# First layer of a two-layer transformer kernel: the gates' arithmetic moved ahead of the first projections, the query blocks ahead of the gate blocks, both running sums together, and the wait for a trip through DRAM left to one queue

## The reference

```
h  = layernorm(x) * (1 + ca) + sa
q, k, v, gate = h @ Wq.T, h @ Wk.T, h @ Wv.T, h @ Wg.T     # 32 query heads, 8 key heads, D = 128; rope on q and k
dt = softplus(h @ Win.T + dt_bias);  g = -dt * exp(A_log_bias)
G  = cumsum(g) inside chunks of 128 tokens
y_intra = (q k^T * causal * exp(G_i - G_j)) (v dt)
state   = state * exp(G_last) + (k exp(G_last - G))^T (v dt)
y_inter = (q exp(G)) state_before
y = rmsnorm(y_intra + y_inter) * gnorm_w * silu(gate);  out = y @ Wo.T
```

## Time and profile before

| What | us |
|---|---|
| median of 3 runs | 1562.36 |
| the three runs | 1556.58, 1562.36, 1563.45 |
| the profiled execution | 1558.13 |
| its span | 1556.3 |

### The profile page before, as it was taken

One profiled execution on the slowest core, in us unless ns is written; L12 is line 12 of the kernel. 1 busy time (PEld: TensorE's weight loads), 2 busy tenths in 40 slices (PEclk: granted clock), 3 DMA queues, 4 the chain that ended last, 5 costly groups with the idle time before them and its releaser, 6 DMA issues. The chain is left out here.

```text
span 1556.3 us, 18582 instructions
## 1 busy us (share of the span) xinstructions
PE 1270.4 (82%) x6079; PEld 896.2 (58%) x6079; DVE 997.4 (64%) x1723; ACT 630.2 (40%) x1177; POOL 736.0 (47%) x742
## 2 busy tenths in 40 slices
PE   4869999999999999999999999776989999951000
PEld 2647767767776777777777777565853334330000
DVE  6635565655655566556656565676578888437888
ACT  2333433433333433433433433245327767734223
POOL 0255755656655756756756756656200012041007
PEclk9989999999999999999999999989868989965555
DMA  4212122122113121121121121120654310000001
GB/s 155 70 49 62 41 76 68 55 69 81 55 55 94 43 69 51 59 68 48 61 69 52 57 68 43 46 95 1 129 109 70 58 38 2 2 1 0 0 0 54
DMA packets 70552, 86.47 MB, mean 56 GB/s; under 512 B 6853, under 2 KB 40805, under 8 KB 69882
## 3 DMA queue, kind: packets, MB, share of 16 engines
q1 hardware_dynamic: 68586, 82.57, 19.6%
q10 hardware_dynamic: 1872, 2.72, 0.5%
HBM read 77.49 MB, written 7.51 MB: 55 GB/s over the span
## 5 line engine op out<-in xcount | busy, mean ns | idle before, releaser
L1657 POOL TENSOR_TENSOR sw<-sw,sinT 128x512 f32<-128x512 f32 x80 | 103.0, 1287 | 153.4 <-ACT sw L1390 153.4
L1190 DVE TENSOR_REDUCE nm<-banks 128x2 f32<-128x1024 f32 x128 | 152.1, 1219 | 33.4 <-PE banks L747 32.8
L1439 ACT ACTIVATE yTh<-yF 128x512 fp32r<-128x512 f32 x64 | 40.4, 631 | 319.2 <-DVE yF L1042 319.2
L1669 POOL TENSOR_TENSOR dec<-gb,gcol 128x512 f32<-128x512 f32 x64 | 70.8, 1107 | 206.7 <-DVE Sd L1008 197.5
L1545 ACT ACTIVATE Pb<-banks 128x512 f32<-128x512 f32 x256 | 135.0, 602 | 52.7 <-PE banks L768 52.2
L545 PE MATMUL banks<-hTh,wgh 128*128 128x512 f32 x256 | 122.5, 479 | 0.0
L980 DVE SCALAR_TENSOR_TENSOR gs<-tg,banks 128x512 f32<-128x512 f32 x64 | 44.0, 687 | 120.8 <-ACT tg L1397 120.8
L597 PE MATMUL banks<-st,qt 128*128 128x128 f32 x384 | 82.4, 299 | 37.1 <-DVE Sd L1008 21.1
L545 PE MATMUL banks<-hTh,wqh 128*128 128x512 f32 x256 | 108.0, 422 | 0.0
L625 PE MATMUL banks<-woh,yTh 128*128 128x512 f32 x256 | 105.0, 410 | 3.5 <-DVE yTl L1045 3.5
L545 PE MATMUL banks<-hTh,wql 128*128 128x512 f32 x256 | 101.7, 397 | 0.0
(11 more groups left out here) (307 smaller groups left out, 3410.4 us busy)
## 6 DMA issues: line engine op xcount, KB each, us to landing
gb<-g_scr SPq DMA_DIRECT2D x64, 256.0 KB, 3.5
raw<-in_wmod SPq DMA_DIRECT2D x40, 256.0 KB, 2.7
raw<-in_wo SPq DMA_DIRECT2D x32, 256.0 KB, 2.9
raw<-in_wq SPq DMA_DIRECT2D x31, 256.0 KB, 2.7
raw<-in_wg SPq DMA_DIRECT2D x31, 256.0 KB, 2.7
qsT<-q_scr SPq DMA_DIRECT2D x24, 256.0 KB, 6.7
q_scr<-hl SPq DMA_DIRECT2D x32, 128.0 KB, 4.3
mt<-mods_scr SPq DMA_DIRECT2D x12, 256.0 KB, 4.9
```

Source lines behind the costliest of these rows:

```text
L1190: ve.tensor_reduce(nm[:, b, i, p:32:16], pairs[z_][:, :].rearrange("p (g t) -> p g t", g=2), AX.X, ALU.max, negate=True).then_inc(*v_nm.up ...
L1657: po.tensor_tensor(s_[:, :], s_[:, :], sinT[:, :], ALU.mult).then_inc(*g_rope.up("sin", kind, t, n))
L1669: po.tensor_tensor(dec[:, :, :], gb[s % 2][:, :, :], bc(gcol[:, t % 2, heads(t), n], 2, 128), ALU.subtract).then_inc(*g_dec.up("sub", s))
```

## The change

The gates are called before the first projections rather than two steps behind one another, so they stand earlier in each queue, above all in DVE's. The query blocks of group 0 come ahead of its gate blocks; gate blocks 2 and 3 go into slot 0. Both running sums are made in one step, with the second in bank 4. The barrier `loop_start` goes on all five engines (DVE's stands for them in the diff): SP waits for the DRAM writes ahead of `load_gb(0)` and `load_gb(4)`, and POOL waits for `gcol`, `dtc` and `cxd` where it reads them. Two instructions add the bias in place of eight. Slot 0 is written out by itself, and the four splits of the output weights go into it. The list of `group_order(0)` follows the new order.

```
     def group_order(g):
         if g == 0:
-            return [("k", 0), ("q", 0), ("v", 0), ("g", 0), ("q", 1), ("g", 1), ("q", 2), ("g", 2), ("q", 3), ("g", 3),
+            return [("k", 0), ("q", 0), ("v", 0), ("q", 1), ("q", 2), ("q", 3), ("g", 0), ("g", 1), ("g", 2), ("g", 3),
+    gbank = (5, 4)
...
-                for i in range(NT):
-                    v = ve.tensor_tensor(z[:, i // 4, :, i % 4], banks[5][:, i * 32:(i + 1) * 32], dtb[:, :], ALU.add)
+                for b in range(2):
+                    v = ve.tensor_tensor(z[:, b, :, :].rearrange("p h n -> p n h"), banks[5][:, b * 128:(b + 1) * 128].rearrange("p (n h) -> p n h", n=4),
+                                         bc(dtb[:, :], 1, 4), ALU.add)
...
-        def loop_start(self):
-            ve = self.e
-            ve.wait_ge(*v_dt("cxd"))
-            ve.wait_ge(*d_gs[0](0))
-            ve.wait_ge(*d_gs[1](0))
...
         def prep(self, s):
             po.wait_ge(*d_gb[s % 2](s))
+            if s == 0:
+                po.wait_ge(*v_dt("gcol", 1))
...
         def load_gb(self, s):
             sp, t, n = self.e, s // 4, s % 4
+            if s in (0, 4):
+                sp.wait_ge(*d_gs[t](0))
...
     def first_pieces(E):
+        E.gate(0), E.gate(1)
+        E.piece("k", 0, 0)
+        E.gate(2)
+        E.split()
+        E.gate(3), E.gate(4)
+        E.piece("q", 0, 0)
+        E.gate(5)
+        E.split()
+        E.piece("v", 0, 0)
+        E.turn_k(0)
+        E.gate(6), E.gate(7)
+        E.piece("q", 0, 1)
+        E.turn_v(0)
+        E.prep2(0, ("xc",))
+        E.split()
+        E.piece("q", 0, 2)
+        E.gsum()
+        E.split()
+        E.piece("q", 0, 3)
+        E.gcols()
+        E.load_gb(0), E.load_gb(1)
+        E.split()
+        E.prep(0)
+        E.piece("g", 0, 0)
+        E.state_cols()
+        E.prep_exp(0)
+        E.prep2(0, ("xd",))
+        E.split()
+        E.piece("g", 0, 1)
+
+    def first_slot(E):
+        E.scores(0)
+        E.prep(1)
+        E.piece("g", 0, 2)
+        E.outputs(0)
+        E.norm_a(0)
+        E.prep_exp(1)
+        E.norm_pow(0)
+        E.piece("g", 0, 3)
+        E.split(), E.split()
+        E.piece("q", 1, 0)
+        E.state(0)
+        E.load_gb(2)
+        E.norm_b(0)
+        E.piece("g", 1, 0)
+        E.split(), E.split()
+        E.piece("k", 1, 0)
+        E.prep2(1)
```

More of the change, by code:

```diff
@@ L511, in z_turn, with gsum, gcols @@
             mm.then_inc(*p_head.up("zT"))
[L513 to L522, removed]
-            pe = self.e
+        def gsum(self):
+            pe = self.e
+            for b in range(2):
+                pe.wait_ge(*v_dt("g", b))
+                pe.transpose(banks[gbank[b]][:, 0:128], zz[:, b, :, :].rearrange("p h n -> p (h n)"), ident).then_inc(*p_head.up("gT", b))
+        def gcols(self):
+            pe = self.e
+            for b in range(2):
+                pe.wait_ge(*v_dt("gsum", b))
+                pe.transpose(banks[gbank[b]][:, 128:256], gT[b][:, :], ident).then_inc(*p_head.up("gcol", b))
             for b in range(2):
@@ L925, in gate @@
                                             op0=ALU.mult, op1=ALU.mult).then_inc(*v_dt.up("g", b))
[L926 to L944, removed]
@@ L946, in gtot, with gsum @@
-        def gtot(self, part):
-            ve = self.e
[L948 to L956, removed]
-            ve = self.e
-            ve.wait_ge(*v_dt("cxd"))
-            ve.wait_ge(*d_gs[0](0))
-            ve.wait_ge(*d_gs[1](0))
+        def gsum(self):
+            ve = self.e
+            for b in range(2):
+                iv = gT[b][:, :].rearrange("p (a c) -> p a c", c=16)
+                ve.wait_ge(*p_head("gT", b))
+                ve.tensor_copy(gin[b][:, :], banks[gbank[b]][:, 0:128]).then_inc(*v_dt.up("gin", b))
+                ve.wait_ge(*v_dt("gin", b))
+                ve.tensor_tensor_scan(gT[b][:, :], rst[:, :], gin[b][:, :], 0.0, ALU.mult, ALU.add).then_inc(*v_dt.up("scan", b))
+                ve.wait_ge(*v_dt("scan", b))
+                ve.tensor_copy(gtot[b][:, 0:8], iv[:, :, 15]).then_inc(*v_dt.up("ends", b))
+                ve.wait_ge(*v_dt("ends", b))
+                ve.tensor_tensor_scan(gtot[b][:, 8:16], rst[:, 1:9], gtot[b][:, 0:8], 0.0, ALU.mult, ALU.add).then_inc(*v_dt.up("upto", b))
+                ve.wait_ge(*v_dt("upto", b))
+                ve.tensor_tensor(iv[:, 1:8, :], iv[:, 1:8, :], bc(gtot[b][:, 8:15], 2, 16), ALU.add).then_inc(*v_dt.up("gsum", b))
@@ new lines, in gcols, with state_cols @@
+        def gcols(self):
+            ve = self.e
+            for b in range(2):
+                ve.wait_ge(*p_head("gcol", b))
+                ve.tensor_copy(gcol[:, b, :, :].rearrange("p h n -> p (h n)"), banks[gbank[b]][:, 128:256]).then_inc(*v_dt.up("gcol", b))
+            ve.wait_ge(*p_head("gtot"))
+            ve.wait_ge(*v_dt("gcol", 1))
+            ve.tensor_tensor(bhn(ww), banks[7][:, 0:256], bhn(gcol), ALU.subtract).then_inc(*v_dt.up("tot"))
+        def state_cols(self):
+            ve = self.e
+            ve.wait_ge(*a_head("tot"))
+            ve.tensor_tensor(bhn(cxd), bhn(ww), bhn(dtc), ALU.mult).then_inc(*v_dt.up("cxd"))
@@ L1853, in send_tile, with gsum @@
             sp.dma_start(raw[k % NRAW][:, :], weight_src(k)).then_inc(*d_raw[k % NRAW].up(k))
-        def gsum(self, b):
+        def gsum(self):
             sp = self.e
[L1857 to L1864, removed]
+            for b in range(2):
+                sp.wait_ge(*v_dt("gsum", b))
+                sp.dma_start(d_g[b], gT[b][:, :]).then_inc(*d_gs[b].up(0))
         def load_gb(self, s):
             sp, t, n = self.e, s // 4, s % 4
+            if s in (0, 4):
+                sp.wait_ge(*d_gs[t](0))
             if s >= 2:
@@ L2348, in layer0_head @@
         E.z_turn()
-        ahead = stream(E, first_pieces)
-        for part in range(8):
-            E.gate(part)
-            if part < 7:
-                ahead.step(), ahead.step()
-        for b in range(2):
-            E.gsum(b)
-            ahead.step(), ahead.step()
-        E.gtot(0)
-        ahead.step(), ahead.step()
-        E.gtot(1)
-        ahead.rest()
-        E.loop_start()
-    def layer0_loop(E):
-        E.load_gb(0), E.load_gb(1)
-        E.prep(0), E.prep_exp(0), E.prep2(0)
-        for _ in range(4):
-            E.split()
-        for s in range(NSLOT - 4):
+    def layer0_loop(E):
+        first_pieces(E)
+        first_slot(E)
+        for s in range(1, NSLOT - 4):
             t, n = s // 4, s % 4
```

52 lines of the change are left out of this document (14 added, 38 removed).

## The result

| | before | changed |
|---|---|---|
| median us (runs) | 1561.83 (4) | 1540.65 (4) |
| lowest, highest | 1556.58, 1563.45 | 1534.91, 1543.67 |
| profiled execution, its span | 1558.13, 1556.3 | 1540.01, 1538.2 |

The ratio is 0.9866, interval 0.9828 to 0.9903: 21 us less, and between 15 and 27. The forecast was 10.3 us less, 1552, range 1545 to 1560.

What follows compares the result with a forecast made beforehand. PE was taken as the bound, busy 82% of the span, with waits and half-speed clock in the head. Removed 20.2, put back 9.7, rounding 0.2: gain 10.3 us, 1562.4 to 1552; range 1545 to 1560, likeliest 1548 to 1556.

Steps and rivals of the forecast that it cites:

- DVE up to the key: Before the key's cos product: reciprocal and one multiplication move into DVE's 2.06 us idle gap; cost nothing.
- From the key to g and the sums: DVE's gate chain in the head, held up by POOL: g at 60.2, first sum at 65.6, second at 69.0.
- The open point about one-input instructions: Whether DVE's one-input SBUF instructions also wait for POOL: counted as free; otherwise some 1.3 us less gain, 1553.
- PE's waits: In the head, PE waits 2.1 us for g and 5.6 us (2.3 and then 3.3) for the sums.
- Clock of the head: Work at half speed behind PE's head waits: nothing counted for the 2.1 us wait, 2.0 us for the 5.6.
- The trip: The sums' way through DRAM to `Sd`, made at 79.8; PE reaches the outputs at 81.4, 1.6 us to spare.
- The exit: From k of group 1 to the first outputs with a state: the old 8.2 us, 4.0 us qt wait stays.
- From slot 1 on the order is the same: The loop behind the head: unchanged order, no gain or loss counted.
- The prediction's own sign of being wrong: Wrong if, among other signs, the end of the loop is not shifted by what slot 1 is.
- The light hold-up: Rival on DVE and POOL in the head: sums by 64 to 65, PE hardly waits; gain 15 to 18, 1546; chance 0.18.
- Slower: Rival: from the wait for g on, PE's clock stays at 0.5; up to 21.8 us cost, 1572; chance 0.04.
- worse hold-up: Rival: DVE and POOL alternate strictly in the head, second sum at 72.8; gain 5.5 us, 1557; chance 0.20.

Runs made afterwards that it cites:

- e_nobar: The kernel before with only the barrier changed: no engine waits for cxd and the DRAM writes but SP and POOL; 1550.8 us, ratio 0.9955.
- e_fill: The changed kernel with idle products of 0.43 us put into PE's waits, in the head and in the loop; 1531.9 us.
- f_a: The changed kernel with idle products in the waits at g, the two sums and qt of slot 1 alone; 1537.7 us.
- f_b: The kernel before with idle products in PE's waits of the head and of slots 0 and 1 alone; 1552.9 us.
- x_before: The kernel before run and profiled once more, no edit; 1559.0 us, ratio 1.002.

## Why the prediction was wrong, point by point

*What bounds the kernel.* Right: PE, with the waits and the falls of the clock as the loss of the head.

*DVE up to the key.* Right: the reciprocal and the product fit into the old gap; cos k starts at 46.82, 4.19 us behind the first gate instruction as before (43.25 to 47.44). The stretch itself began 0.6 us earlier, in front of anything that was changed; such shifts are between -1.5 and +0.7 us in the profiles of the kernels, so it is not the change's.

*From the key to g and the sums.* Right in kind, a little too long. Counted from the same start, g came at 59.7 of my 60.2 and the second sum at 67.8 of 69.0. DVE's hold-up by POOL is there. The open point about one-input instructions is decided, against my choice: the scale took 1.27 us beside POOL's addition of 48.30 to 49.59, and the 128x8 copy at 61.76 took 0.84. Before, beside an idle POOL:

```profile
54.66 0.29 DVE L909 TENSOR_SCALAR pz<-pz 128x256 f32<-128x256 f32 x1
71.87 0.17 DVE L938 COPY gtot<-gT 128x8 f32<-128x8 f32 x1
```

The Trainium skill, "SBUF — State Buffer", section "Who interferes with whom", says that copies and scalings can enter a mode that takes both ports and then contend with GpSimd, and the trace agrees. The reciprocal, also with one input, was not held: 1.74 us beside POOL before, 1.75 at 44.52 beside an idle POOL. The hold-up of the scale is 1.0 us. What it cost the chain is not measured by itself; g came no later than forecast.

*PE's waits.* 6.1 us in place of 7.7 (1.5 and 4.6 for 2.1 and 5.6). *Clock of the head.* 2.2 in place of 2.0. *The trip.* Right: hidden, `Sd` ready 1.5 us ahead of PE (forecast 1.6). *The exit.* Right: 99.76 - 91.60 = 8.16, and the 4.0 us wait stayed. Up to the scores of slot 1 the gain is 13.0, of which 0.6 is the earlier start: 12.4 against 10.3, mainly since the waits came out 1.6 shorter. Slot 1's own fall was then 1.3 longer, so 11.8 at slot 8.

*The step that failed* is "From slot 1 on the order is the same" with its price of nothing. The order is the same and so are the waits, but each of the seven 3.0 us waits is followed by a fall or not. By the marks the loop took 5.8 us less (by the windows its falls cost 10.9 us before and 4.7 after), of the 18.1 us of the profiled pair. I had called the loop "bound by PE" at a clock of 0.99: a hundredth there is one fall of 1.6 us in these 230 us, and I counted it as nothing, and gave 0.03 to a loss by the clock later and no chance to a gain. The prediction's own sign of being wrong came: the end of the loop is shifted by 17.6 us and not by the 13.0 of slot 1.

The rest is the step from profile to median, where I had added 4.2 us and kept the difference. The profiled execution of before was 3.7 us below its median, that of the changed kernel 0.6, which adds 3.1 us to the first comparison. Over all runs the kernel before stands at 1557.8 and not at the 1562.4 of its first three. So 1552 was 4.6 us too high at its base and had a gain 8.7 us too small (10.3 for 19.0).

*The luck in it.* The head did what the change was meant for, 12 to 13 us. The shorter loop, 6 to 7 us in the profiles, was not meant by any part of the change. It comes from the place at which the new head lets the loop meet the clock's grid, and in e_nobar an edit worth 0.6 us at the head got the same.

*The rivals.* The light hold-up, 1546, came nearest, but for a wrong reason: the sums came at 67.1, not at 64 to 65, and PE waited 6.1 us. Slower and worse hold-up did not come.

**What is shown and what is not.** Shown: the falls hang on PE's waits (e_fill), and their sum makes the loop's length to 0.7 us. Shown: the loop's falls change with the head though no instruction of the loop does (the median of e_nobar is 6.0 us lower, its head 0.6 to 1.3 us shorter), and the changed kernel had the short loop in three profiles of three; its 16 runs are all below 1545. Read from the profiles, one execution for each label: the falls go in the main with the place of slot 8 on the grid, and the head's falls hand the loop that place; the spread of f_a's times supports it, that of f_b's does not. Open: what makes one place cost three falls and another six. Nothing here would have let one forecast it from the profile of before.

## What to carry to other kernels

Where PE waits near 3 us again and again, the clock's answer is part of the time, and it changes with any edit ahead of it: price each such wait with and without a fall of 1.6 us, put the sum into the range on both sides, and compare marks in the trace (one instruction per slot) before a gain is put down to an edit. Better still, remove the waits: the change won 19 us of 1558, 12 to 13 of them at the head, and together with two moves in the queues of POOL and DVE and idle products in three waits it won 64. In a queue that runs in order, an instruction with a long wait in front of it belongs behind the ones that the critical engine needs; and DVE's instructions with two inputs in SBUF wait for POOL's, as do a scale (1.27 us for 0.29) and a copy (0.84 for 0.17) with one; the reciprocal did not.

## What was not expected of the hardware

The falls of a profile all begin and end on one grid of equal steps. In the profile of before the four falls between 70 and 120 us begin 3, 4 and 5 steps behind one another and last 1, 2, 1 and 1. Where this grid lies against the start of the span differs in each execution: by 0.33, 0.57, 0.77 and 0.54 of a step in the four profiles with the old head and its barrier.

Two executions of one kernel thus get falls behind different slots (x_before and before), with every wait of the loop alike, 2.96 to 2.97 us or 1.57 to 1.61. Over 94 executions the kernel before differs by up to 20 us (1543.8 to 1563.6); how much of this is the loop's falls can't be told without their profiles. With the waits filled, six executions spread by 5 us (1529.6 to 1534.9).
